# Two levels of block multiplication for half of the batches, with the weight sums prepared beside the first half

## The reference

```python
x = x + (x @ B0[i0].T) @ A0[i0].T            # rank 16
y = x + x @ W + (x @ A1[i1]) @ B1[i1]        # W is 2048 x 2048, rank 16
```

## Time and profile before

| | us |
|---|---|
| runs (3) | 1402.41, 1403.8, 1404.17; median 1403.8 |
| the profiled execution's own time | 1402.34 |
| its span | 1400.7 |
| PE busy | 1367.2 (98%) |
| DVE busy | 810.2 (58%) |
| ACT busy | 405.9 (29%) |
| DMA | 261.81 MB, mean 187 GB/s |

### The profile page before, as it was taken

How to read it: one execution, slowest core, us unless ns; L and a number is a source line. 1 busy time by engine, 2 the same in 40 slices (tenths; PEclk the granted TensorE clock), 3 DMA queues, 4 the chain that set the end, 5 groups by cost and what they waited for, 6 DMA issues and landing times.

```text
span 1400.7 us, 15653 instructions
## 1 busy us (share of the span) xinstructions
PE 1367.2 (98%) x6016; PEld 1129.2 (81%) x6016; DVE 810.2 (58%) x941; ACT 405.9 (29%) x462; POOL 165.0 (12%) x317
## 2 busy tenths in 40 slices
PE   5999999999999999999999999999999999999997
PEld 4888888888878888888887888888887888888886
DVE  3455855357776455646775555555766445554675
ACT  2332222223234223322332323232322422232230
POOL 3200100111123010012011010012012001001202
PEclk8999999999999999999999999999999999999999
DMA  8864843458887343357684252446785334234755
GB/s 303 310 225 134 299 158 113 153 186 280 294 280 240 122 136 120 129 195 246 236 289 146 86 173 96 151 151 213 256 297 187 99 120 135 91 91 133 223 201 180
DMA packets 76778, 261.81 MB, mean 187 GB/s; under 512 B 12176, under 2 KB 12176, under 8 KB 76576
## 3 DMA queue, kind: packets, MB, share of 16 engines
q1 hardware_dynamic: 57600, 205.55, 43.5%
q0 software_dynamic: 19104, 55.27, 11.7%
HBM read 213.52 MB, written 48.30 MB: 187 GB/s over the span
## 4 chain that ended last, share of the span: by engine, by line
PE 85%; DVE 5%; DMA 5%; ACT 2%; issue 2%; POOL 0%; POOLq 0%; SPq 0%; ACTq 0%; DVEq 0%
PE y_ps L1024 76%; PE lr_ps L955 4%; PE p_ps L997 3%; DMA w_raw<-in_W 2%; PE y_ps L976 2%; ACT w_hi L555 2%; DVE w_lo L708 1%; DVE w_raw L694 1%; DVE b_lo L721 1%; DMA w_raw<-w_sum 1%; DVE u L776 1%; DMA stage_all<-lrw 0%; DMA u<-in_A0n 0%; DVE u L777 0%; DVE val L835 0%
## 5 line engine op out<-in xcount | busy, mean ns | idle before, releaser
L1024 PE MATMUL y_ps<-b_hi,w_hi 128*128 128x512 f32 x1792 | 699.3, 390 | 15.3 <-DVE w_lo L708 8.8
L1024 PE MATMUL y_ps<-b_lo,w_hi 128*128 128x512 f32 x1792 | 698.6, 390 | 0.0
L1024 PE MATMUL y_ps<-b_hi,w_lo 128*128 128x512 f32 x1792 | 698.4, 390 | 0.0
L708 DVE TENSOR_TENSOR w_lo<-w_raw,w_hi 128x1024 fp32r<-128x1024 f32 x216 | 264.6, 1225 | 460.9 <-ACT w_hi L555 460.9
L555 ACT CAST w_hi<-w_raw 128x1024 fp32r<-128x1024 f32 x216 | 227.6, 1054 | 879.5 <-PE y_ps L1024 474.9
L1024 PEld LDWEIGHTS y_ps<-b_hi,w_hi 128*128 128x128 f32 x1792 | 337.3, 188 | 86.6 <-DVE w_lo L708 8.8
L1024 PEld LDWEIGHTS y_ps<-b_hi,w_lo 128*128 128x128 f32 x1792 | 337.2, 188 | 70.2
L1024 PEld LDWEIGHTS y_ps<-b_lo,w_hi 128*128 128x128 f32 x1792 | 337.3, 188 | 70.1
L721 DVE TENSOR_TENSOR b_lo<-x_raw,b_hi 128x1024 fp32r<-128x1024 f32 x112 | 136.5, 1219 | 0.0
L566 ACT CAST b_hi<-x_raw 128x1024 fp32r<-128x1024 f32 x112 | 117.5, 1049 | 2.4 <-DMA x_raw<-in_xT 2.4
L694 DVE TENSOR_TENSOR w_raw<-w_raw 128x1024 f32<-128x1024 f32 x64 | 78.1, 1221 | 19.5 <-DMA w_raw<-in_W 11.6
(11 more groups left out here) (81 smaller groups left out, 605.8 us busy)
## 6 DMA issues: line engine op xcount, KB each, us to landing
w_raw<-in_W SPq DMA_DIRECT2D x208, 512.0 KB, 3.8
w_raw<-w_sum SPq DMA_DIRECT2D x96, 512.0 KB, 3.6
x_raw<-in_xT SPq DMA_DIRECT2D x64, 512.0 KB, 5.4
out_y<-u POOLq DMA_DIRECT2D x64, 256.0 KB, 6.4
out_y<-stage_all POOLq DMA_DIRECT2D x64, 256.0 KB, 3.4
lr_raw<-lrw POOLq DMA_DIRECT2D x64, 128.0 KB, 4.0
w_sum<-w_raw SPq DMA_DIRECT2D x8, 512.0 KB, 6.2
c_kept<-stage_all POOLq DMA_DIRECT2D x16, 256.0 KB, 3.2
```

The costliest lines, as they stand in the source:

```text
L708: dve.tensor_tensor(w_lo[n % 2][:, :, :], w_tile(n)[:, :, :], w_hi[n % 2][:, :, :].bitcast(F32), ALU.subtract).then_inc(w_ready, 1)
L1024: last = pe.matmul(bank[:, :], w[n % 2][:, c, t * P:(t + 1) * P], x[:, 2 * j + c, :], start=(j == 0 and c == 0 and w is w_hi and x is b_hi ...
```

## The change

The last four batches are computed as one problem with two levels. Outer level: x as 2 x 2 blocks of (half of the contraction, pair of batches), W in 1024 x 1024 quarters, products M1, M2, M7, M6, M4, M3, M5. Inner level: each outer product, 1024 x 1024 by 1024 x 1024, is split again into seven products Q1, Q2, Q6, Q5, Q7, Q3, Q4 of 512 x 512 by 512 x 512, each of two units of 24 matmuls. Q1, Q6, Q7 and Q4 form a chain: they go on adding in the same four PSUM banks, and their contents are read out after each. The other three use two further banks in turn. Outer results are collected in `uq` and `stage`; some are added to the output in HBM by DMAs that accumulate.

The first four batches keep the one-level form in two pairs, 112 units. During them, the inner sums of weights are prepared: 14 jobs (outer product, half of the columns), each with four loads of 512 KB blocks, four sums on VectorE and four stores to `w_ops`. GpSimd issues the loads and the stores. Ten jobs use three tiles in the memory of `a0_hi`, `a0_lo` and `q1`, and two and two use `x_raw` tiles that have become free. The sums of P3 and P5 of pair 0 are kept as well (`store_kept`), and pair 1 loads them instead of adding again. The x21 loads of pair 1 move from P4 of pair 0 to P1 of pair 1. The two id loads move from GpSimd to the head of SP's list. W is laid out with 4 KB or 1 KB rows for the two kinds of loads, the output with pairs of tiles beside each other.

The diff, cut to its core (the functions of the first part that only moved into `one_level` are left out):

```diff
...
+S2, S3, F3, F5 = range(4)
...
+M1, M2, M7, M6, M4, M3, M5 = range(7)
+Q1, Q2, Q6, Q5, Q7, Q3, Q4 = range(7)
+Q_UNITS = 14
+CHAIN = (Q1, Q6, Q7, Q4)
+C11, C12, C21, C22 = range(4)
+ADDS = {Q1: ((C11, True),), Q2: ((C11, False),), Q6: ((C12, True),), Q5: ((C12, False), (C22, True)),
+        Q7: ((C22, False),), Q3: ((C12, False),), Q4: ((C21, True),)}
+LAST_OF = {C11: Q2, C12: Q3, C22: Q7, C21: Q4}
+W_QUARTER = {Q1: (0, 0), Q2: (0, 1), Q4: (1, 1)}
+X_TILE = {Q1: 0, Q2: 1, Q6: 0, Q5: 0, Q7: 2, Q3: 3, Q4: 1}
+X_QUARTER = (0, 2, 1, 3)
+W_BLOCK = {M1: A11, M2: A12, M4: A22}
+W_SUM = {M7: S3, M6: S2, M3: F3, M5: F5}
+X_BLOCK = {M1: (0, 0), M2: (1, 0), M7: (0, 1), M6: (0, 0), M4: (1, 0), M3: (1, 1), M5: (1, 1)}
+IN_OF = (M1, M2, M7, M3)
+IN_Q = (Q1, Q2, Q7, Q3)
+SLOT = {Q1: 0, Q2: 0, Q7: 1, Q3: 1}
+GROUP = {M2: (0, 1, 0, 0), M7: (1, 0, 1, 1), M4: (0, 1, 0, 0), M5: (1, 0, 1, 1)}
+FIN = {4: (C11, 0), 5: (C11, 1), 9: (C22, 0), 10: (C22, 1), 11: (C12, 0), 12: (C12, 1), 13: (C21, 0),
+       14: (C21, 1)}
...
-        return (o in (P1, P4, P5) or (p, o) == (0, P6)) and u // 4 == u % 4 // 2
+        return (o in (P1, P4) or p == 0 and o in (P6, P5)) and u // 4 == u % 4 // 2
...
-        return o in (P3, P5) or (p, o) == (0, P6)
+        return p == 0 and o in (P6, P3, P5)
...
+    def keep_use(n):
+        p, o, u = at(n)
+        return UNITS * (o == P5) + u if p == 0 and o in (P3, P5) else None
...
+    halves = [(o, h) for o in (M2, M1, M7, M6, M4, M3, M5) for h in range(2)]
+    jobs = [(*halves[i], 0, unit(0, P3, 2) + 6 * i) for i in range(10)]
+    jobs += [(*halves[10 + i], 1, unit(1, P7, 2) + 8 * i) for i in range(2)]
+    jobs += [(*halves[12 + i], 2, unit(1, P4, 2) + 8 * i) for i in range(2)]
+    ta, tc, td, tb = range(4)
+    JOB_AT = {ta: (0, 0), tc: (1, 0), td: (1, 1), tb: (0, 1)}
+    js3, js1, js2, js4 = range(4)
+    JOB_SUM = {js3: ta, js1: tc, js2: td, js4: tb}
+    def job_tile(s, t):
+        return (s, ta if s == 0 and t == tb else t)
+    job_loads, job_sums, job_stores = {}, {}, {}
+    for i, (_, _, s, n) in enumerate(jobs):
+        for t, late in ((tc, 0), (td, 0), (ta, 1 if s == 0 else 0), (tb, 4 if s == 0 else 0)):
+            job_loads.setdefault(n + late, []).append((i, t))
+        for k, late in ((js3, 2), (js1, 2), (js2, 3), (js4, 5 if s == 0 else 3)):
+            job_sums.setdefault(n + late, []).append((i, k))
+            job_stores.setdefault(n + late + 1, []).append((i, k))
...
+        def load_job(i, t):
+            o, h, _, _ = jobs[i]
+            tile, s, _ = job_use(i, t)
+            for pair in job_tile_free(i, t):
+                pool.wait_ge(*pair)
+            row, col = JOB_AT[t]
+            if o in W_SUM:
+                block = w_sum[W_SUM[o]]
+                for u in (4 * row + 2 * col, 4 * row + 2 * col + 1):
+                    pool.wait_ge(*sum_kept(W_SUM[o], u))
+            else:
+                block = W[W_BLOCK[o]]
+            pool.dma_start(tile, half_of(block, row, col, h)).then_inc(job_loaded[s], 16)
+        def store_job(i, k):
+            o, h, _, _ = jobs[i]
+            tile, s, t = job_use(i, JOB_SUM[k])
+            pool.wait_ge(job_summed, job_no[i, k])
+            pool.dma_start(w_ops[o, k, :, h, :, :], tile).then_inc(job_stored[s][t], 16)
...
+            for i, k in job_stores.get(n, []):
+                store_job(i, k)
+            for i, t in job_loads.get(n, []):
+                load_job(i, t)
+            early(n)
...
+            if p and i == X21:
+                sp.wait_ge(w_ready, unit(0, P5, 4 + j) + 1)
+                sp.wait_ge(f_stored[j], 16 * 4)
...
+            kind = {P7: S3}.get(o) if p == 0 else {P6: S2, P7: S3, P3: F3, P5: F5}.get(o)
...
+        def store_kept(n):
+            use = keep_use(n)
+            sp.wait_ge(presum_done, presums.index(n) + 1)
+            sp.dma_start(unit_of(w_sum[F5 if use >= UNITS else F3], use % UNITS), w_tile(n)
+                         ).then_inc(f_stored[use % 4], 16)
...
+        sp.dma_start(ids[:, 0, :], shared.ids0).then_inc(ids_loaded, 16)
+        sp.dma_start(ids[:, 1, :], shared.ids1).then_inc(ids_loaded, 16)
+        load_x(0, X11, 0)
...
+        def job_sum(i, k):
+            o, h, s, _ = jobs[i]
+            a, c, d, b = (job_use(i, t)[0] for t in (ta, tc, td, tb))
+            if k == js3:
+                dve.wait_ge(*job_loaded_for(i, ta))
+                dve.wait_ge(*job_loaded_for(i, tc))
+                if o in (M1, M4):
+                    job_eye(a, h)
+                dve.tensor_tensor(a, c, a, ALU.subtract).then_inc(job_summed, 1)
+            elif k == js1:
+                dve.wait_ge(job_summed, job_no[i, js3])
+                dve.wait_ge(*job_loaded_for(i, td))
+                if o in (M1, M4):
+                    job_eye(d, h)
+                dve.tensor_tensor(c, c, d, ALU.add).then_inc(job_summed, 1)
+            elif k == js2:
+                dve.wait_ge(job_summed, job_no[i, js1])
+                dve.tensor_tensor(d, d, a, ALU.add).then_inc(job_summed, 1)
+            else:
+                dve.wait_ge(job_summed, job_no[i, js2])
+                dve.wait_ge(*job_loaded_for(i, tb))
+                dve.tensor_tensor(b, b, d, ALU.subtract).then_inc(job_summed, 1)
+        eyes = [0]
+        def job_eye(tile, h):
+            for col in range(2):
+                part = tile[:, 2 * h + col, col * P:(col + 1) * P]
+                last = dve.tensor_tensor(part, part, eye[:, :], ALU.add)
+            last.then_inc(job_eyed, 1)
+            eyes[0] += 1
+            dve.wait_ge(job_eyed, eyes[0])
...
+    def early_sums(n):
+        if not 0 <= n < LAST:
+            return []
+        mo, u = at(n)
+        out = []
+        if u == 0 and x_worked(mo, 1):
+            out.append(("xq", mo, 1))
+        if u == 4:
+            out.append(("t1", mo))
+        return out
+    def late_sums(n):
+        if not 0 <= n < LAST:
+            return []
+        mo, u = at(n)
+        out = []
+        if mo < M5:
+            for v, i in ((8, 0), (10, 2), (12, 3)):
+                if u == v and x_worked(mo + 1, i):
+                    out.append(("xq", mo + 1, i))
+            if u == 13:
+                out.append(("t3", mo + 1))
+        if n == 0:
+            out.append(("t3", M1))
+        if u == 1:
+            out.append(("t2", mo))
+        if u == 2:
+            out.append(("t4", mo))
+        return out
...
+    def evicts(n, part):
+        if part == 0:
+            n -= 1
+        if not 0 <= n < LAST:
+            return []
+        po = n % Q_UNITS // 2
+        q, h = n // 2, n % 2
+        if po in CHAIN:
+            return [(q, 2 * h, 2, c, begins) for c, begins in ADDS[po]] if part == 0 else []
+        return [(q, 2 * h + 1 - part, 1, c, begins) for c, begins in ADDS[po]]
+    def by_act(q, begins):
+        return begins and product(q)[0] in (M1, M7, M4, M5)
...
+        def store_stage(mo, c, h):
+            g, m = GROUP[mo][c], 4 * (c // 2) + 2 * h
+            one_pair, other = batch(0, c % 2), batch(1, c % 2)
+            tiles, stored = stage[:, g, 2 * h:2 * h + 2, :], stage_stored[g][h]
+            pool.wait_ge(*quarter_done(mo, c, 2 * h + 1))
+            if mo == M2:
+                pool.dma_start(y_at(one_pair, m), tiles).then_inc(stored, 16)
+            elif mo == M7:
+                pool.dma_start(y_at(other, m + 8), tiles).then_inc(stored, 16)
+                pool.dma_start(y_at(one_pair, m + 8), tiles).then_inc(stored, 16)
+            else:
+                pool.wait_ge(u_stored[c], 16 * 4)
+                pool.dma_start(y_at(other if mo == M5 else one_pair, m + 8), tiles, accum_op=ALU.add
+                               ).then_inc(stored, 16)
+        def store_u2(c, h):
+            m = 4 * (c // 2) + 2 * h + 8
+            pool.wait_ge(*quarter_done(M6, c, 2 * h + 1))
+            pool.wait_ge(stage_stored[GROUP[M7][c]][h], 16 * stage_stores(M7, c, h))
+            for pair in (1, 0):
+                pool.dma_start(y_at(batch(pair, c % 2), m), uq[:, c, 2 * h:2 * h + 2, :], accum_op=ALU.add
+                               ).then_inc(u_stored[c], 16)
...
+        def load_w(q):
+            mo, po = product(q)
+            tile = wq[q % WEIGHTS]
+            if q >= WEIGHTS:
+                sp.wait_ge(*w_split_done(q - WEIGHTS))
+            else:
+                sp.wait_ge(x_ready, 4 * (PRODUCTS + P3) + 4)
+            if po in W_QUARTER:
+                i, j = W_QUARTER[po]
+                if mo in W_SUM:
+                    block = w_sum[W_SUM[mo]]
+                    for u in (4 * i + 2 * j, 4 * i + 2 * j + 1):
+                        sp.wait_ge(*first.sum_kept(W_SUM[mo], u))
+                else:
+                    block = W[W_BLOCK[mo]]
+                for h in range(2):
+                    sp.dma_start(tile[:, h, :, :], half_of(block, i, j, h)).then_inc(w_loaded[q % WEIGHTS][h], 16)
+            else:
+                k = {Q7: 0, Q5: 1, Q6: 2, Q3: 3}[po]
+                for h in range(2):
```

(52 more changed lines are left out.)

2462 lines of the change are left out of this document (1679 added, 783 removed).

## The result

The changed kernel takes 1454.7 us (median of 4 runs, 1451.71 to 1458.86), the kernel before 1403.99 on the same chip. The ratio is 1.0371, with a 95% interval of 1.0349 to 1.0393: slower. The forecast was 1386 with a range up to 1422, so it was wrong in sign and in range. The profiled execution took 1452.41 us with a span of 1450.8.

A forecast was written before the change was run, and what follows sets the result against it. TensorE's matmuls were taken to bound the kernel: 1400.7 - 73.8 - 5 + 35 + 6 + 17 + 3 = 1382.9 us of span, and 1386 us as the median of runs. The range was 1345 to 1422.

The forecast's parts named there:

- What bounds the kernel: Whole kernel before the change: TensorE is busy 1367.2 of 1400.7 us, so matmuls are the price; DMA is the second view.
- the matmuls: Both parts: net 332 matmuls fewer at 0.2222 us each, -73.8 us; 5684 matmuls in all.
- the start: Kernel start: id loads on SyncE let GpSimd's A0 loads begin some 5 us earlier; -5 us, between 0 and -10.
- Traffic while the sums are made: P3 and P5 of pair 0, P1 of pair 1: 66.8 MB in 642 matmuls at 375 GB/s, 178 us, +35.
- Late loads reach TensorE through w_lo: First part's job stages: VectorE waits for job loads in its own order, delaying TensorE's weights; no separate size.
- Units 82 to 98: Late first part: 50 job transfers, 402 GB/s needed, 0 to +16; VectorE some 10.8 us in a 5.33 us unit; together +6.
- The ring: First ten jobs: three tiles' dependent transfers take 4L + 5 us in 32 us, deciding from L = 7 us; rival's chance 0.25.
- case B: Slower rival, first part: job ring and late GpSimd DMAs; 1427, or 1412 with half the later six spared, 1415 taken; chance 0.25.
- Second part, +17 for a full VectorE: Second part: VectorE takes over in M5 (+8), level in M6 (+5), tight in M2 and M3 (+2 each); 8 to 30.
- the sign that was named for the accumulating stores: Second part: M6 losing more than M5 would make the prediction wrong and point to the accumulating stores.
- 0 taken, +32 kept for the range: M7 and M6: 12.6 MB accumulate in HBM; moved twice they make 193 us (+32), but 0 entered the sum.
- Handover and tail: Boundary between parts and kernel end: one boundary replaces two, the end gains a copy, closing sum and two stores; +3, -2 to +8.

## Why the prediction was wrong

- **What bounds the kernel, the matmuls, the start: right.** 5684 matmuls; 332 x 0.2247 is 74.6 us, not 73.8. The first p_ps matmul starts at 20.83 instead of 24.67 us, and of that 2.6 us are left at P4's end (296.8 against 299.4): -2.6 for -5, inside the 0 to -10. But this mark lies anywhere from 296.3 to 299.9 in the other kernels with the same start, so what is shown is 0 to 3 us.
- **"Traffic while the sums are made", +35: the mechanism right in the main, the size wrong.** This step failed first in time. From 300 to 500 us the kernel before starts 864 matmuls and the changed one 644: 49 us. The bytes were right (64.0 MB for 644 matmuls, 66.8 forecast for 642). The rate was not: 375 GB/s assumed, 320 measured over the stretch, so 200 us and not 178. It was exceeded only where the queues were full (401 to 413 GB/s at 404 to 412 us). A share of 0.92 at 320 makes 348 at full, so about half of the shortfall is engines without work, and half a lower full rate. The sum divided bytes by one rate, as if the engines always had work. But a job's fourth load may only be issued when its first sum is stored, and each stop of VectorE empties the queues. "Late loads reach TensorE through w_lo" stood in the text, and had no price; but that is the smaller part, for 63 of the 91 us that the first part loses stay when VectorE does not wait for job loads at all.
- **Units 82 to 98, +6: the largest miss of the first part.** Between 620 and 810 us, which are these units and those up to 112, 700 matmuls start where 845 would: 33 us. VectorE's 10.8 us of work in a unit was priced, not that it stands 13.25 us at a job load in front of it. That load was issued only when VectorE came to wait for it, at 666.42 us: GpSimd had spent 5.92 us on issuing eight other transfers and waited twice for output tiles before. That units 64 to 82 lose nothing was right (524 starts from 500 to 620 us, 531 without jobs).
- **The ring as a rival only.** It was to decide from L = 7 us. Job loads from W landed in 8.8 (median), but their stores in 4.5, so the four landings and 5 us make 31.6 us in a ring of 32: no slack, and a stop with every landing that is longer, as that of 14 us above. Its 82 us for the first part is near the 91 measured, less what was lost before, and that is luck: it had 30 us for six jobs past unit 66, and from 500 to 620 us nearly nothing is lost, while 41 of the jobs' 68 us come without VectorE's waits. The two 3.8 and 6.4 us landings on which it was weighed come from a trace that is mostly calm, which the text itself says. The error was to hold traffic and ring as alternatives: fuller queues lengthen L, and the ring turns L into stops. And case B's 1415 halved the later price for no reason that a row gave (and the halved sum is 1412); unhalved it was 1427.
- **Second part, +17 for a full VectorE: not seen.** The 2048-column difference took 2.285 us (2.28 assumed). But VectorE is busy for 69.1 of the 90 us from 1350 to 1440 us, which lie in M5, where over 95% was the sign; what M5 loses goes in large part with the later joins (178 starts become 206 in the stretch at 550 us). With plain stores the second part still loses 28 us; less the 10 of the joins this is near 17, but by luck. And M6 loses most and not M5, the sign that was named for the accumulating stores. **"0 taken, +32 kept for the range"** is the second step that failed: they cost 26 us, and moving the bytes twice, the mechanism named for the 32, is near the 1.9 that GpSimd's queue shows. The range, up to 1422, took in the 32 alone (1418) and case B as halved (1415), but not B's 1427, and not the two together: 1427 and 26 make 1453. That this meets the measured time is luck too, for B's parts were wrong in place.
- **A held bank was not seen.** The joins keep a side bank until val is split; moving them one unit gives 10 us alone.
- **Handover and tail, +3: right.** From the last matmul to the end it is 11.1 us against 9.1.
- **The Trainium skill.** By HBM Reference, Specifications (TRN2), a core alone goes well above 358 GB/s: 401 to 413 over 8 us agree, and 320 as the mean of 200 us with dependent transfers in them shows that such a rate is not what a stage gets. By 358 the prediction had +44, nearer to the 49 measured than +35, but only one core runs here, so the figure fits for another reason than the page's. The contention that GPSIMD Engine Reference, Specifications, names was put as a support of case B. That it would make the DMAs of GpSimd land late was the prediction's own step, and no run here shows it: with SyncE issuing the job loads landed in 7.9 us instead of 8.8, which speaks for full queues. The direction was case B's; the reason of this page was not shown.

A smaller slip of reading: in slices 9 to 12 VectorE has 5, 7, 7, 7 tenths and DMA 186 to 294 GB/s, not 7 or 8 tenths and 280 to 294; nothing in the sum rests on it.

What stays open: how the 41 us of transfers without VectorE's waits divide between rate and GpSimd's own in-order waits (22 of them fall in 300 to 500 us, where the engines are full, the rest later), and why the lrw loads behind P3's first val come late in every version that was read there (140 to 151 starts from 300 to 340 us, 175 before), with or without jobs and kept sums.

## What to carry to other kernels

Work that is to run in the shade of an engine needs a check of its longest dependent chain at the landing time of the full stage, not of the calm mean, and of what stands behind each wait on an in-order engine. Bytes through a full rate give only the lower end of its price; where chain time and period are near each other, add the two and count the stop, the emptied queues and the half clock after it. And a term whose row is missing goes into the sum at the value that its mechanism gives, not at zero because the range holds the rest.

## What the runs showed of the hardware

- Stores that accumulate in HBM make full DMA engines move less: 246 GB/s at a share of 1.06 against 354 at 0.93 with plain stores in the same 44 us, 1.9 times the engines' time for a megabyte of the queue that carries them; 26 us of the kernel for 40 such stores, 21.0 MB, 12.6 of them in M6.
- Two issues of SyncE took 12.52 us while the queues were full, with no wait between them in the code, where one took 0.38 or 0.42 us in the kernel before. With plain stores, at a share of 0.93, four took 10.75 us and six 23.30.
- 512 KB loads of the kernel's own W tiles landed in 7.8 us (median of 88) against 3.8 before, with 242 GB/s over the span against 187.
